# Biased attention on one core: queries and keys laid with one partition half per sequence, scores in four array quadrants

## Time and profile before

| | us |
|---|---|
| median of 3 runs | 2077.37 |
| lowest, highest | 2075.01, 2078.09 |
| profiled execution | 2080.65 |
| its span, first to last instruction | 2078.8 |
| mean granted TensorE clock | 0.966 |

### The profile page before, as it was taken

The page is one execution under the profiler, slowest core; times in us unless marked ns, Lnnn a source line. Parts: engine busy times, 40 slices in busy tenths (PEclk is TensorE's granted clock), DMA queues, the critical chain, the costliest instruction groups (busy, mean ns, idle before and its releaser), DMA issues. The chain is left out here.

```text
span 2078.8 us, 43922 instructions
## 1 busy us (share of the span) xinstructions
PE 1908.7 (92%) x17090; PEld 1391.3 (67%) x17090; DVE 1252.1 (60%) x2923; ACT 889.0 (43%) x1679; POOL 679.0 (33%) x797
## 2 busy tenths in 40 slices
PE   4999999989999999999999999289978999999877
PEld 2566666667888888887665687166655777777643
DVE  5566666537666676766332222277756777777767
ACT  1433334445555555554222233165633444444334
POOL 2111111113333333333135200565503444444446
PEclk8899999999999999999899999599989999999999
DMA  8000000000000000000100022201100000000001
GB/s 283 1 2 0 0 0 0 1 1 1 1 0 0 0 0 0 0 0 1 71 23 26 17 90 84 58 25 22 17 2 1 2 2 0 0 0 1 2 11 30
DMA packets 31324, 40.28 MB, mean 19 GB/s; under 512 B 5225, under 2 KB 25501, under 8 KB 30708
## 3 DMA queue, kind: packets, MB, share of 16 engines
q1 hardware_dynamic: 27124, 32.00, 4.7%
q0 software_dynamic: 4096, 6.83, 1.6%
HBM read 28.33 MB, written 12.06 MB: 19 GB/s over the span
## 5 line engine op out<-in xcount | busy, mean ns | idle before, releaser
L153 POOL TENSOR_TENSOR rstd<-var_eps,minus_half 128x2 f32<-128x2 f32 (+1 forms) x116 | 92.7, 799 | 457.2 <-DVE var_eps L147 411.4
L974 POOL TENSOR_TENSOR xa_probs<-xa_probs,xa_total 128x512 f32<-128x512 f32 x128 | 133.3, 1041 | 196.5 <-DVE xa_total L1040 191.9
L1045 DVE TENSOR_REDUCE xa_top<-ps 128x4 f32<-128x512 f32 x128 | 88.0, 688 | 120.6 <-PE ps L818 119.5
L477 ACT ACTIVATE la_hid<-ps,pack_moe 128x512 f32<-128x512 f32 x128 | 87.8, 687 | 144.6 <-PE ps L309 143.5
L930 ACT ACTIVATE xa_probs<-xa_probs 128x512 f32<-128x512 f32 x128 | 80.7, 631 | 157.2 <-DVE xa_probs L1048 157.2
L2109 PE MATMUL ps<-ba_inT,pack_latent 128*128 128x256 f32 x512 | 141.4, 403 | 3.0 <-ACT ba_inT L2227 1.4
L807 PEld LDWEIGHTS ps<-xa_kvT,xa_qk_fold 128*128 128x128 f32 x512 | 96.5, 190 | 64.2 <-issue 41.6
L818 PE MATMUL ps<-xa_kvT,xa_qT 128*128 128x128 f32 x1024 | 135.2, 275 | 0.0
L834 PE MATMUL ps<-xa_probsT,xa_kv 128*128 128x512 f32 x256 | 133.3, 602 | 2.1 <-ACT xa_attnT L939 1.8
L309 PE MATMUL ps<-la_h2T,pack_moe 128*128 128x512 f32 x256 | 131.6, 628 | 0.4 <-ACT la_hid L477 0.4
L807 PE MATMUL ps<-xa_kvT,xa_qk_fold 128*128 128x256 f32 x512 | 130.7, 380 | 0.2 <-ACT xa_kvT L897 0.2
(11 more groups left out here) (312 smaller groups left out, 4222.2 us busy)
## 6 DMA issues: line engine op xcount, KB each, us to landing
expert_weights<-experts_dram SPq DMA_DIRECT2D x8, 768.0 KB, 4.6
slot_rows<-zeros SPq DMA_DIRECT2D x1, 2560.0 KB
expert_rows<-slot_rows SPq DMA_DIRECT2D x8, 320.0 KB, 2.9
result_rows<-ex_result SPq DMA_DIRECT2D x8, 320.0 KB, 2.4
pack_moe<-moe_dram SPq DMA_DIRECT2D x1, 2312.0 KB
pack_latent<-latent_dram SPq DMA_DIRECT2D x1, 2050.0 KB, 20.0
pack_latent<-biased_dram SPq DMA_DIRECT2D x1, 2048.0 KB, 7.9
out_dram<-X SPq DMA_DIRECT2D x8, 256.0 KB, 2.3
```

Of the source, the lines that this page charges most:

```text
L153: pool.tensor_tensor(m.rstd[:, 0:tiles], m.var_eps[:, 0:tiles], m.minus_half[:, 0:tiles], ALU.pow).then_inc(sem.rstd, 1)
L477: act.activation(hid[:, n // F0 % 2, n % F0, :], HIDDEN[n % 2], ACT.Silu, bias=w["b1"][:, n:n + 1]).then_inc(hid_ready, 1)
L974: pool.tensor_tensor(probs[:, u % 4], probs[:, u % 4], over(total[:, u % 4], 2, KEYS), ALU.mult).then_inc(probs_ready, 1)
L1045: dve.tensor_reduce(top[:, s % 4], scores, AX.X, ALU.max).then_inc(top_ready, 1)
```

```diff
-        qT = sb("qT", [P, 2, HP, NS])
-        kT = sb("kT", [P, 2, HP, NS])
+        qT = sb("qT", [P, 2, H, P])
+        kT = sb("kT", [P, 2, H, P])
...
-                return (qT, kT)[n // 4][:, k, 2 * (n % 4):2 * (n % 4) + 2, :].rearrange("p h n -> p (h n)")
+                return (qT, kT)[n // 4][:, k, 4 * (n % 4):4 * (n % 4) + 4, :].rearrange("p h n -> p (h n)")
...
-                        for h in range(2):
-                            hp = 2 * (n % 4) + h
-                            mm = pe.matmul(proj_bank(n)[:, NS * h:NS * h + NS], (w["bq"], w["bk"])[n // 4][:, P * hp:P * hp + P],
-                                           inT[:, n // 4, :], start=True, stop=True)
+                        tokens = inT[:, n // 4, :].rearrange("p (t b q) -> p b t q", t=2, b=2)
+                        for h in range(4):
+                            at = DHX * (4 * (n % 4) + h)
+                            for b in range(2):
+                                mm = pe.matmul(proj_bank(n)[SEQ * b:SEQ * b + SEQ, P * h:P * h + P],
+                                               (w["bq"], w["bk"])[n // 4][:, at:at + DHX], tokens[:, b], start=True, stop=True)
...
+                    at = slice(SEQ * t, SEQ * t + SEQ)
                     for n in range(UH):
                         for b in range(2):
+                            part = slice(SEQ * b, SEQ * b + SEQ)
                             for par in range(2):
-                                part = slice(DHX * par, DHX * par + DHX)
-                                at = slice(P * t + SEQ * b, P * t + SEQ * b + SEQ)
-                                mm = pe.matmul(bank(u % 2)[SEQ * par:SEQ * par + SEQ, P * n + SEQ * b:P * n + SEQ * b + SEQ],
-                                               qT[part, k, UH * half + n, at], kT[part, k, UH * half + n, at],
-                                               start=True, stop=True)
+                                head = 2 * (UH * half + n) + par
+                                mm = pe.matmul(bank(b)[SEQ * par:SEQ * par + SEQ, SEQ * n:SEQ * n + SEQ],
+                                               qT[part, k, head, at], kT[part, k, head, at], start=True, stop=True)
...
+                        if here:
+                            reach(pe, masked, count(step, UNITS, s))
                         if ahead >= 1:
                             projection(later(step, 1), PER_SLOT * s + 1)
...
-                            dve.tensor_tensor(by_head(s), bank(s % 2).rearrange("p (h k) -> p h k", k=SEQ),
-                                              over(scaled_mask[:], 1, 2 * UH), ALU.mult).then_inc(masked, 1)
+                            dve.tensor_tensor(probs[:, s % 4].rearrange("p n b k -> p b n k"),
+                                              m.ps[:, 0:2, 0:UH * SEQ].rearrange("p b (n k) -> p b n k", k=SEQ),
+                                              over(over(scaled_mask[:], 1, UH), 1, 2), ALU.mult).then_inc(masked, 1)
```

## The result

The changed kernel takes 2082.11 us (median of 15 runs, 2077.67 to 2085.52) against 2076.51 of the kernel before (15 runs): a ratio of 1.0021, interval 1.0014 to 1.0029. Forecast were 2064.4 and a clear gain; it is 5.6 us slower, and outside the range. The profiled execution took 2083.78 us, its span 2081.9.

The account below looks back on a forecast made before the run. PE was taken to bound the loop, 98.4% busy. Cheaper scores less dearer banks and shape changes gave 0.86 us a step, 13 us over 15 steps: 2077.4 - 13 = 2064.4, range 2048 to 2075.

Parts of the forecast that it names:

- scores in four quadrants: Score units: 8 rounds of four for 16 of two, 0.63 us for 1.08, 1.80 less a step.
- half-width banks and shape changes: Query and key projections: a bank 1.04 us for 0.86 in full width, plus changes between full and small shapes.
- sum of a step: PE's pieces added over slots 0 to 3: 0.86 us less a step, about 13 us over 15 steps.
- what bounds the kernel now: In the loop PE, busy 98.4 of 100 us, sets a step's length; its pieces are priced from start to start.
- four rivals: Free small-shape changes (2046), unhidden loads (2112), gain lost to waits (2073 to 2078), half quadrant gain or dearer banks (2077 or 2069).
- Rival 2: Query and key banks: half-width blocks' loads are not hidden, a step 2.3 us longer, 2112; chance 0.10 including worse.
- The banks: Query and key projections as 16 instructions of 128x64, 8 rounds of two: 1.04 to 1.08 us, taken as 1.04.
- The shape changes: PE between unlike tile shapes: each change pays a fixed cost, 0.14 between small shapes; the turned unit becomes 0.63.
- rival 1: Changes between the two small shapes are free: 2.06 us saved a step, 2046; chance 0.13 including values up to the forecast.
- The new wait on `masked`: PE's wait for DVE's masking before a projection: costs nothing until masking is 2.9 us late; masking stays 0.69.
- bank 8: Value bank in slot 2, needing ACT's copy of bank 6: room shrinks from 0.34 to 0.07 us, further savings lost.
- turned unit: Transposes between projections in slots 0 to 2: 0.63 us for 0.43, from going to full width and back.

Follow-up runs that it names:

- experiment 4: Changed kernel with the two full-width matmuls of before in each query and key bank, leaving only the scores' change: 0.9882 of the kernel before.
- experiment 1: Changed kernel with PE's loop written out, no jump back, other engines keeping their loops: 0.9933 of the kernel before; run once more, 0.9925.
- experiment 5: Kernel before, only longer: score matmuls of three of four head pairs cut into two of 32 columns each; 1.0359 of the kernel before.

## Why the prediction was wrong

From first to sixtieth score unit, each part measured by leaving it out:

| part | forecast, us | measured, us | from |
|---|---|---|---|
| scores in four quadrants | -27.0 | -22.0 | 377.2 to 355.2 (experiment 4) |
| half-width banks and shape changes | +14.1 | +7.8 | 355.2 to 363.0 (1 against 4) |
| code fetched at four jumps back | none | +19.1 | 363.0 to 382.1 (after against 1) |
| sum | -13 | +4.9 | |

**The step that failed** stands in the sum of a step and in "what bounds the kernel now": I took PE's time as the sum of its pieces and never asked how many instructions the loop's body has, so fetching its code stood in the sum at nothing, without a reason. The runs showed 19.1 us for it. The change was described with "each query and key projection is four times as many matmuls"; the matmuls' time was priced, their number was not. The trace of before held the hint: no DMA at all in the middle of the loop, while the page counts 73 instruction packets in the whole execution, so the body was being kept, and something had to be its limit. None of the four rivals had it. Rival 2 ended on the side where the result lies, but its mechanism is not there.

**What held.** The scores: a unit 0.62 to 0.63, forecast 0.63. The banks: 1.02 to 1.03, forecast 1.04. The shape changes are paid between all pairs, 128x64 to 64x64 among them: rival 1 falls. The new wait on `masked` costs nothing, and DVE's masking stays at its length. The one place where I said a further saving would be lost is bank 8, and it was: from score to bank 8 it is 0.62 to 0.64 in the changed kernel, but 0.73 in every step of experiment 1, where the copy of bank 6 had ended only 0.15 before, and 0.73 to 0.80 in experiment 4. I had left it 0.07 of room; so 0.11 us a step of the gain without the holes is already lost there.

**Sizes that were off.** Scores, -22.0 for -27.0: a step inside the loop saves 1.66, since bank 8's copy takes part of it back, and the first two steps save only 0.3 and 0.9, while I gave all 15 the full amount. Banks and shapes, +7.8 for +14.1: a bank is 1.02 and not 1.04, the turned unit of slot 0 is 0.59 and not 0.63, and the longer bank in front of `turn_top` costs nothing, since PE waits there anyway. The turned unit of slot 1 takes 0.53, but the output projection in front of it takes 1.89 for 1.79, so together they cost what was summed. Both errors nearly cancel, and that is luck: without the holes the kernel is at 0.9933 and 0.9925 of before, 14 to 16 us, for 13 forecast.

**Rival 2's rule.** The loads of half-width blocks are hidden behind matmuls on the same rows; the 16 instructions of a bank start in pairs 0.109 apart, and with the prediction's 0.05 for an unhidden load in each of its 8 rounds a bank would take over 1.4 (an estimate). The rule on row groups that rival 2 quotes from the Trainium skill (TensorE: Matmul & The Clock Gate, Part 3) does not hold here.

## What to carry to other kernels

Where a change cuts matmuls into smaller ones inside a hardware loop, count the instructions of the loop's body before the cycles: past some 1700 on PE (1723 was kept, 1851 was not) every jump back cost 4 to 10 us here, part of it as idle time and part as work at half the granted clock behind it. Look at the instruction queue in the middle of the loop: here every loop without packets had no hole at its jump, and every loop with packets in each pass had one. The cure was to write the loop out (0.993 of before, the fastest kernel here that computes all of the reference); a prefetch hint got two thirds of it, since one hole of 5 us then stands at the way out. And a bank of matmuls that seems to stand in the wrong place may be the cover of two waits; where the order is changed, price what the work that moves away leaves behind.

## What the runs showed of the hardware that I had not expected

- Straight code is fetched without a visible cost, although PE runs some 37 instructions in a microsecond (3680 matmuls and loads in 100 us at 98% busy in experiment 1); what is paid stands at the loop's branch, at the jump back or, with the hint, at the way out.
- The hole varies from pass to pass (4.0 to 5.9 in the changed kernel, 5.1 to 9.7 in experiment 5), though PE's idle time in it hardly does (3.2 to 3.5). What varies is the granted clock behind it: 0.50 behind three of four jumps in the one and behind all four in the other, 1.00 behind the shortest hole (3.22 idle). What decides whether it falls isn't shown.
- With a hint for the jump, the same body (1857 records with the hint) stayed on the chip: no fetch in the loop after the first pass.
- Score rounds of 32 columns save next to nothing against 64: cutting three quarters of the 64 rounds of a step in two made the step 2.8 us longer, 0.059 for each round more, and 0.059 is what a round of 64 columns costs in the prediction.
